# Holding up-projection blocks in PSUM and rounding all sigmoid pieces on ScalarE in a one-core FFN kernel

## The reference, cut to what matters

```python
def act_qdq(x):
    scale = jnp.maximum(jnp.max(jnp.abs(x)) / qmax, 1e-12)      # qmax = 32767
    return jnp.clip(jnp.round(x / scale), -qmax - 1.0, qmax) * scale
def fixed_qdq_u16(x):
    return jnp.clip(jnp.round(x * 65536), 0.0, 65535.0) / 65536
x = act_qdq(x)                                    # (16, 128, 128): 2048 tokens of 128
up = act_qdq(x @ lpbq_dequant(w_up).T)            # 384 wide
gate = act_qdq(x @ lpbq_dequant(w_gate).T)
sig = fixed_qdq_u16(jax.nn.sigmoid(gate))
gate = act_qdq(gate * sig)
o = act_qdq(gate * up)
return o @ lpbq_dequant(w_down).T
```

## Time and profile before

| | |
|---|---|
| Median of 3 runs | 301.76 us (301.69 to 303.23) |
| Span of the profiled execution, first to last instruction | 301.2 us |
| Median less this span | 0.56 us |
| TensorE busy | 264.4 us (88%) |
| VectorE busy | 258.8 us (86%) |
| ScalarE busy | 215.6 us (72%) |
| GpSimd busy | 76.2 us (25%) |
| Chain that ended last | TensorE 79%, VectorE 16% of the span |

### The profile page before, as it was taken

How to read it: one execution, slowest core, us unless ns; L and a number is a source line. 1 busy time by engine, 2 the same in 40 slices (tenths; PEclk the granted TensorE clock), 3 DMA queues, 4 the chain that set the end, 5 groups by cost and what they waited for, 6 DMA issues and landing times.

```text
span 301.2 us, 8834 instructions
## 1 busy us (share of the span) xinstructions
PE 264.4 (88%) x2716; PEld 205.5 (68%) x2716; DVE 258.8 (86%) x635; ACT 215.6 (72%) x455; POOL 76.2 (25%) x148
## 2 busy tenths in 40 slices
PE   4969940049989999999999999999999999999994
PEld 4824440016956777778888788888777887888874
DVE  4888999989898897779988799887799988889885
ACT  6367899998842677767777676667566766689892
POOL 3367997000025413011302112212110311101000
PEclk9989976557999999999999999999999999999999
DMA  6990443101500000000000000000001000001000
GB/s 186 314 310 4 84 94 76 28 0 35 90 17 2 0 3 1 0 2 2 19 0 0 2 3 26 2 0 0 1 2 30 8 0 0 2 1 37 0 2 27
DMA packets 24031, 10.63 MB, mean 35 GB/s; under 512 B 13355, under 2 KB 22982, under 8 KB 24006
## 3 DMA queue, kind: packets, MB, share of 16 engines
q1 hardware_dynamic: 23470, 10.05, 13.6%
q10 hardware_dynamic: 536, 0.26, 0.3%
HBM read 6.11 MB, written 1.05 MB: 24 GB/s over the span
## 4 chain that ended last, share of the span: by engine, by line
PE 79%; DVE 16%; issue 1%; ACT 1%; DMA 1%; SPq 0%; DVEq 0%
PE bank L893 78%; DVE peak L706 3%; DVE big L728 3%; DVE peak L633 2%; DVE big L711 1%; DVE big L744 1%; PE bank L937 1%; DMA y_sb<-in_cond 1%; PE bank L1017 0%; DVE big L746 0%; DVE wyT L779 0%; DVE pkm L626 0%; DVE big L738 0%; DVE x_sb L759 0%; DVE q L700 0%
## 5 line engine op out<-in xcount | busy, mean ns | idle before, releaser
L893 PE MATMUL bank<-big,wt 128*128 128x384 f16 (+2 forms) x480 | 124.8, 336 | 0.6 <-DVE big L872 0.5
L893 PE MATMUL bank<-wt,big 128*128 (+1 forms) x1536 | 111.5, 219 | 0.1
L872 DVE TENSOR_TENSOR big<-big 128x384 f16<-128x384 f32 (+2 forms) x160 | 93.2, 585 | 20.5 <-ACT big L594 16.1
L893 PEld LDWEIGHTS bank<-wt,big 128*128 128x128 f16 x1536 | 97.9, 97 | 16.2 <-issue 0.2
L592 ACT ACTIVATE big<-bank,miscT 128x384 f32<-128x384 f32 (+2 forms) x160 | 96.2, 602 | 15.3 <-PE bank L893 8.2
L893 PEld LDWEIGHTS bank<-q,wxh 128*128 128x128 f32 x254 | 44.4, 189 | 17.4 <-issue 3.4
L893 PEld LDWEIGHTS bank<-big,wt 128*128 (+1 forms) x480 | 50.0, 117 | 4.8 <-issue 1.1
L580 ACT ACTIVATE q<-bank (+1 forms) x112 | 20.6, 184 | 38.7 <-PE bank L893 37.9
L404 POOL CAST big<-q 128x64 f16<-128x64 f32 x32 | 13.2, 413 | 129.0 <-ACT q L580 126.5
L868 DVE CAST big<-big 128x512 f16<-128x512 f32 (+2 forms) x104 | 38.6, 372 | 4.8 <-ACT big L592 3.9
L827 DVE SCALAR_TENSOR_TENSOR wyT<-bank,gates,wyT 128x128 f32<-128x128 f32 x128 | 39.8, 343 | 1.0 <-issue 0.6
(11 more groups left out here) (165 smaller groups left out, 320.0 us busy)
## 6 DMA issues: line engine op xcount, KB each, us to landing
wnat<-in_w SPq DMA_DIRECT2D x8, 512.0 KB, 7.7
x_sb<-in_x SPq DMA_DIRECT2D x4, 256.0 KB, 4.3
out_block<-wyT SPq DMA_DIRECT2D x15, 64.0 KB
wn<-in_w_gate ACTq DMA_DIRECT2D x1, 192.0 KB, 4.9
wn<-in_w_up SPq DMA_DIRECT2D x1, 192.0 KB, 5.6
wn<-in_w_down SPq DMA_DIRECT2D x1, 192.0 KB, 5.7
b_in<-in_b SPq DMA_DIRECT2D x12, 4.0 KB
wt<-wyT SPq DMA_TRANSPOSE x8, 3.0
```

The source lines that it names most:

```text
L872: V.tensor_tensor(g_lo[:, par, f, 0:w], g32[:, f, 0:w], g_hi[:, par, f, 0:w], ALU.subtract).then_inc(g_lo_done, 1)
L893: return nc.tensor.matmul(o, l, r, start=start, stop=stop, skip_group_check=True)
```

## The change

- Only the first 17 of the 24 projection blocks are copied out by ScalarE. The last seven, up blocks m = 5 to 11, stay in banks 0, 1, 2, 5, 6, 3 and 4 (`HELD_BANKS`). VectorE takes their maxima from there, one by one; ScalarE rounds them out of the bank into `up2`.
- All six sigmoid pieces are rounded by ScalarE; `round_sigmoid` on VectorE is gone, and so the up scale has no `meanwhile`.
- Up is rounded in six pieces of 1024; a piece with a held block takes two instructions of 512, ten in all. VectorE's products wait for their own piece.
- TensorE's transposes of x come after the last up piece and behind `spread_peak(3)`, and `take_xT` stands between the later roundings on ScalarE. The Gelu table is loaded after these.
- `weight_lo(2)` on VectorE comes right after the gate scale, and TensorE's block 23, which goes to its bank 4, waits for it.

```diff
@@ -54,8 +54,9 @@
 CHUNK_OF = [c for c in range(CH) for _ in range(TILES[c])]
 LAST_SYNC, LAST_SCALAR = (0, 2), (1,)
 LATE = NK - ACC_SCALAR
-SIG_V = 2
 B2_ROWS = CTILES * E
+UP_OUT = 5
+UP_HELD = NJ * NK - UP_OUT
 GATE_UP = 2.0 ** 18
 
 
...
@@ -179,6 +180,7 @@
         DOWN_BANKS = [1, 2, 3, 4, 5]
         ACC_BANKS = [6, 7, 1, 2]
         GU_BANKS = [5, 6, 0, 1, 2]
+        HELD_BANKS = [GU_BANKS[(NJ * NK + m) % 5] if m < 10 else 3 + m - 10 for m in range(UP_OUT, NJ * NK)]
         W0_BANKS = [4, 3, 4]
         W_BANKS = [0, 5]
         MISC_AT = NJ * P
@@ -208,6 +210,18 @@
 
         def sixth(t, n):
             return t[:, TOK // 2 * n:TOK // 2 * (n + 1)]
+
+        def up_bank(m):
+
+            return banks[HELD_BANKS[m - UP_OUT]]
+
+        def up_pieces():
+
+            return [[(b, b % NK * NJ + b // NK) for b in (2 * n, 2 * n + 1)] for n in range(2 * NJ)]
+
+        def up_steps(n):
+
+            return sum(1 if all(m < UP_OUT for _, m in piece) else len(piece) for piece in up_pieces()[:n])
 
         def tokens(t, k):
 
@@ -500,7 +514,7 @@
                 A(blk(qhi, k), c32[:, 4 * k:4 * k + 4, :].rearrange("p b l -> p (b l)"), ACT.Copy,
                   bias=-MAGIC).then_inc(q_hi_s, 1)
 
-            for n in range(2 * NJ * NK):
+            for n in range(NJ * NK + UP_OUT):
                 act.wait_ge(gu_mm, n + 1)
                 t, k, j = (gate2, up2)[n // (NJ * NK)], n % (NJ * NK) // NJ, n % NJ
                 A(blk(t, j * NK + k), banks[GU_BANKS[n % 5]][:, :], ACT.Copy).then_inc(gu_sb, 1)
@@ -516,22 +530,24 @@
                 A(sixth(gate2, n), sixth(gate2, n), ACT.Copy, scale=sc[:, 1, 4:5], bias=MAGIC).then_inc(gateq, 1)
                 act.wait_ge(gateq, n + 1)
                 A(sixth(sig2, n), q16(sixth(gate2, n)), ACT.Sigmoid, scale=sc[:, 1, 2:3]).then_inc(sig_done, 1)
-                if n >= SIG_V:
-                    act.wait_ge(sig_done, n + 1)
-                    A(q16(sixth(sig2, n), U16), sixth(sig2, n), ACT.Copy, scale=65536.0).then_inc(sig_16, 1)
+                act.wait_ge(sig_done, n + 1)
+                A(q16(sixth(sig2, n), U16), sixth(sig2, n), ACT.Copy, scale=65536.0).then_inc(sig_16, 1)
 
             act.wait_ge(scale_done, 3)
-            for n in range(NJ):
-                A(third(up2, n), third(up2, n), ACT.Copy, scale=sc[:, 2, 4:5], bias=MAGIC).then_inc(upq, 1)
-            nc.scalar.preload_act_table(ACT.Gelu)
-            for k in range(2):
-                take_xT(k)
+            for n, piece in enumerate(up_pieces()):
+                if all(m < UP_OUT for _, m in piece):
+                    A(sixth(up2, n), sixth(up2, n), ACT.Copy, scale=sc[:, 2, 4:5], bias=MAGIC).then_inc(upq, 1)
+                    continue
+                for b, m in piece:
+                    src = blk(up2, b) if m < UP_OUT else up_bank(m)[:, :]
+                    A(blk(up2, b), src, ACT.Copy, scale=sc[:, 2, 4:5], bias=MAGIC).then_inc(upq, 1)
 
             act.wait_ge(scale_done, 4)
             for n in range(1, 2 * NJ):
                 A(sixth(sig2, n), sixth(sig2, n), ACT.Copy, scale=sc[:, 3, 4:5], bias=MAGIC).then_inc(g2q, 1)
-                if n <= 2:
-                    take_xT(n + 1)
+                if n <= NK:
+                    take_xT(n - 1)
+            nc.scalar.preload_act_table(ACT.Gelu)
             act.wait_ge(wt_t[0], 16 * W_POOL)
             weight_hi(W_POOL)
             for i in range(W_POOL, W_CHUNKS - 1):
@@ -706,33 +722,34 @@
                 link(V.tensor_reduce(peak[:, i, k:k + 1], tokens((gate2, up2)[i - 1], k), XY, ALU.max,
                                      apply_absolute_value=True))
 
-            def round_sigmoid(n):
-                dve.wait_ge(sig_done, n + 1)
-                V.tensor_scalar(sixth(sig2, n), sixth(sig2, n), SIG_MAX, SIG_MAGIC, ALU.min, ALU.add).then_inc(sig_round, 1)
-
-            for i in (1, 2):
-
-                for k in range(i - 1, NK):
-                    peak_gate_up(i, k)
-                    if i == 1 and k == 0:
-                        weight_lo(1)
-                    if i == 2 and k == 2:
-                        weight_lo(2)
-                peak_to_scale(i, NK, lambda u: link(V.tensor_scalar(u, sc[:, 0, 2:3], 1.0 / WS, None, ALU.mult)),
-                              (lambda: peak_gate_up(2, 0)) if i == 1 else (lambda: round_sigmoid(0)))
+            def peak_up(first, to):
+                for m in range(first, to):
+                    dve.wait_ge(gu_mm, NJ * NK + m + 1)
+                    link(V.tensor_reduce(peak[:, 2, m - 3:m - 2], up_bank(m)[:, :], X, ALU.max,
+                                         apply_absolute_value=True))
+
+            for k in range(NK):
+                peak_gate_up(1, k)
+                if k == 0:
+                    weight_lo(1)
+            peak_to_scale(1, NK, lambda u: link(V.tensor_scalar(u, sc[:, 0, 2:3], 1.0 / WS, None, ALU.mult)),
+                          lambda: peak_gate_up(2, 0))
+            weight_lo(2)
+            dve.wait_ge(gu_sb, NJ * NK + UP_OUT)
+            link(V.tensor_reduce(peak[:, 2, 1:2], tokens(up2, 1)[:, 0:2, :], XY, ALU.max, apply_absolute_value=True))
+            peak_up(UP_OUT, NJ * NK)
+            peak_to_scale(2, 2 + UP_HELD, lambda u: link(V.tensor_scalar(u, sc[:, 0, 2:3], 1.0 / WS, None, ALU.mult)))
 
             for n in range(2 * NJ):
-                if 0 < n < SIG_V:
-                    round_sigmoid(n)
-                dve.wait_ge(*((sig_round, n + 1) if n < SIG_V else (sig_16, n - SIG_V + 1)))
+                dve.wait_ge(sig_16, n + 1)
                 V.tensor_tensor(sixth(sig2, n), q16(sixth(gate2, n)), q16(sixth(sig2, n), U16), ALU.mult).then_inc(g2_done, 1)
                 dve.wait_ge(g2_done, n + 1)
                 block_peak(3, n, sixth(sig2, n))
             peak_to_scale(3, 2 * NJ, lambda u: link(V.tensor_scalar(u, sc[:, 1, 2:3], 1.0 / 65536.0, None, ALU.mult)))
 
             link(V.tensor_scalar(sixth(sig2, 0), sixth(sig2, 0), sc[:, 3, 4:5], MAGIC, ALU.mult, ALU.add))
-            dve.wait_ge(upq, NJ)
             for n in range(2 * NJ):
+                dve.wait_ge(upq, up_steps(n + 1))
                 if n > 0:
                     dve.wait_ge(g2q, n)
                 V.tensor_tensor(sixth(up2, n), q16(sixth(sig2, n)), q16(sixth(up2, n)), ALU.mult).then_inc(p_done, 1)
@@ -949,7 +966,9 @@
                     pe.wait_ge(*((q_hi_s, Q_HI_SCALAR.index(k) + 1) if k in Q_HI_SCALAR else (q_hi_v, k + 1)))
                 if n == 4:
                     pe.wait_ge(cq_done, 3)
-                if n >= 5:
+                if n == 2 * NJ * NK - 1:
+                    pe.wait_ge(wT_done, 3)
+                if 5 <= n < NJ * NK + 10:
                     pe.wait_ge(gu_sb, n - 4)
                 if n == W0_AT[1]:
                     pe.wait_ge(cq_done, NK)
@@ -959,16 +978,16 @@
                 if n == NJ * NK + 6:
                     spread_peak(1)
                 w = NJ * t + j
-                mm3(banks[GU_BANKS[n % 5]][:, :], wT_hi[:, w, :], wT_lo[:, w, :], blk(qhi, k), blk(qlo, k),
+                o = banks[GU_BANKS[n % 5]] if n < NJ * NK + UP_OUT else up_bank(n - NJ * NK)
+                mm3(o[:, :], wT_hi[:, w, :], wT_lo[:, w, :], blk(qhi, k), blk(qlo, k),
                     r_lo_ready=(q_done, k + 1) if t == 0 and j == 0 else None).then_inc(gu_mm, 1)
-            pe.wait_ge(gu_sb, 2 * NJ * NK)
             spread_peak(2)
-            pe.wait_ge(wT_done, 3)
+            spread_peak(3)
+            pe.wait_ge(upq, up_steps(2 * NJ))
             for k in range(NK):
                 for b in range(4 * k, 4 * k + 4):
                     last = nc.tensor.transpose(banks[1 + k][:, P * (b % 4):P * (b % 4 + 1)], x_sb[:, b, :], ident[:, :])
                 last.then_inc(xT_mm, 1)
-            spread_peak(3)
 
             def keep_busy(n):
 
```

More of the change, by code:

```diff
@@ L159, in program @@
         pk_part, pk_all, scale_done, dve_step, pool_step = sems("pk_part pk_all scale_done dve_step pool_step")
-        gu_mm, gu_sb, gateq, upq, sig_done, sig_round, sig_16, g2_done, g2q, p_done, oq, o_hi_done, o_lo_done, o_lo_p = sems(
-            "gu_mm gu_sb gateq upq sig_done sig_round sig_16 g2_done g2q p_done oq o_hi_done o_lo_done o_lo_p")
+        gu_mm, gu_sb, gateq, upq, sig_done, sig_16, g2_done, g2q, p_done, oq, o_hi_done, o_lo_done, o_lo_p = sems(
+            "gu_mm gu_sb gateq upq sig_done sig_16 g2_done g2q p_done oq o_hi_done o_lo_done o_lo_p")
         down_mm, x1_done, x1_hi_done, x1_lo_done, x1T_mm = sems("down_mm x1_done x1_hi_done x1_lo_done x1T_mm")
```

## The result

The changed kernel took 305.03 us in the median of 7 runs (303.96 to 306.75), the kernel before 302.41 on the same chips (301.69 to 303.23): a ratio of 1.0077, 95% interval 1.0054 to 1.0100. By the ratio it is slower by 2.3 us (the medians lie 2.6 apart), against +0.8 forecast, and 305.03 lies above the stated range, which ended at 304.5.

A forecast was written before the change was run, and what follows sets the result against it. The start of TensorE's weight chunks, where warming and ScalarE's first `weight_hi` meet, was taken as the bound. ScalarE's -3.0 + 2.7 + 0.9 + 0.1 + 0.1 = +0.8 on 301.76 gave 302.6 us, range 301.0 to 304.5.

The forecast's parts named there:

- meeting point: Start of TensorE's weight chunks, which need ScalarE's first `weight_hi`: 72.2 to 72.3 forecast against 71.39, +0.8 to +0.9 us.
- rival A: VectorE's chain sets the end, if ScalarE reaches `weight_hi` before 70 us: at best 300.6 us; chance 0.10.
- steps 1 to 3: ScalarE: seven PSUM copies go, -3.0 us; two more sigmoid roundings, +2.7; up in ten instructions, +0.9, through at 62.9.
- step 4: ScalarE's five roundings and four copies of x, 7.13 us, start at 62.9; the scale they need stands at 62.1.
- 0.8 us of slack: On ScalarE, between the scale of gate times sigmoid at 62.1 and the start of the roundings needing it at 62.9.
- step 5: ScalarE's Gelu table load, 1.28 us, moves behind the roundings and copies of x at the same cost; +0.12 for waiting.
- rival C: The table load on ScalarE costs more in its new place, a second cost of that size: +2.1, 303.9 us; chance 0.06.
- The sum's last step: Eight TensorE chunks at the old pace put the spread of the last maximum at 80.4; the +0.8 reaches the end.
- Rival B: TensorE idles 2.9 us after warming and falls to the lower clock as chunks start: 303.9 to 305.2 us; chance 0.18.

The follow-up runs named there:

- the kernel before with the three moves: The kernel before with the first two high halves made early, Gelu table loaded after the second low byte, 8 warming matmuls: 302.47 us, ratio 1.0001.

## Why the prediction was wrong

Point by point, with after's numbers against the forecast:

- *What bounds the kernel.* Right. The meeting point, start of the weight chunks, decided, and rival A (VectorE's chain) didn't: VectorE idled 4.80 us for the spread, and moving the start of the chunks alone, with VectorE's work as it was, took the whole loss away.
- *ScalarE, steps 1 to 3.* Right to 0.1 us: gate rounding 0.04 behind its scale (34.06, 34.10); six trips 34.10 to 55.39, 21.3; up pieces through at 62.20, 6.8 us.
- *ScalarE, step 4.* Failed in the profiled execution. "0.8 us of slack" was a wait of 0.67. VectorE's maxima were right (40.89 - 30.85 = 10.0 against 9.1, +0.93 for +0.83), but the products took 60.73 - 42.97 = 17.8 instead of 16.3. I had kept the overlap cost with GpSimd at what the old positions gave, 1.87, 1.51 and 1.51; in their new position they gave 1.94, 2.21 and 2.21, and in the execution with more warming 1.39, 1.51 and 2.21, near the forecast: that position is partly chance. The prediction named these multiplications only as a possible gain.
- *ScalarE, step 5, and rival C.* The load took 1.28 and the next instruction began 0.01 after it. C is refuted, and no second cost stands in either place. Nor does a drain of 1.38 us, which the Trainium skill, in "ScalarE: Activation LUTs", What ACT_TABLE_LOAD costs, counts with each load; the 1.28 us of the load itself agree.
- *TensorE.* The transposes ran from 62.26, warming from 65.43 at the full clock (0.95 in the slice from 65 us), after 19 us of idle and then only the two matmuls of a spread and those transposes. That speaks against what the Trainium skill says in "TensorE: Matmul & The Clock Gate", Part 4, of transpose mode, for these fp32 transposes; the rows call them MATMUL, and no row shows the mode.
- *Meeting point.* +1.4 measured in the profiled pair, for +0.8 forecast; the difference is step 4's wait. In the execution with more warming, where ScalarE didn't wait, it was +1.0. This part of the sum was mis-sized by little.
- *The sum's last step* failed, and it is the step that made the forecast wrong: "eight chunks at the old pace". (Six of the eight stand before the spread; the pace, 8.2 us for them, was read rightly.) They took 11.3 us in the profiled execution, since TensorE idled 3.50 us before them and its clock had fallen to 1.2 GHz. Rival B had the mechanism, the place (idle from 68.6 to 72.1) and the price (2.6 at most; 3.1 in the profiled execution), with a chance of 0.18. It should have been the likeliest case. The argument against it, that a late rise shortens the idle, was weak: by its own sum TensorE was free from 69.3 and ScalarE late by up to 2.9 us. And the 2.8 us of idle that B leaned on came from one row; a fall followed 1.90 us in another kernel. In the median the clock's share is 1.0 us, taken as what more warming gave back.
- *The base.* 301.76 was the median of three; the kernel before stood at 302.41 with the changed kernel's runs and at 302.6 to 302.7 in all later sets.

## What to carry to other kernels

Warm-up work on TensorE and the arrival of its first input must end together: here an input that came 1.4 us later cost 3.1 us more behind it, since TensorE idled and then began its real work at half clock. Before moving work onto an engine, ask what stands at the end of its queue and who waits for that; here two instructions, moved ahead of a block they didn't depend on, were worth all 2.3 us, and neither shift of work between ScalarE and VectorE paid, alone or together. A price read beside another engine's work holds only at that position, and the position itself moved by 1 us between executions of the same code.

## What the runs showed of the hardware

VectorE's two-input product and GpSimd's subtraction, both with their operands in SBUF, take turns: 1.22 us alone, 2.21 when it meets a whole subtraction, 1.39 to 1.51 when it meets the end of a step of GpSimd's, and GpSimd's 0.62 becomes 1.59. VectorE's reductions beside such subtractions kept their 1.22 (in the kernel before, the one at 49.54 beside the subtraction at 50.06). The Trainium skill says the same in "SBUF — State Buffer", SBUF: two separate sides: a port pair that GpSimd and a VectorE instruction with two SBUF inputs hold for a whole instruction, the other blocking. The trace agrees: the product at 46.20, begun 0.03 us behind a subtraction of 1.15, took 0.99 us more than alone, and the reductions, with one input, weren't hit.

The granted clock rose to 2.4 GHz near 65.0 us, 2.8 us after the transposes began, in the changed kernel, and 4.8 us after they began in the run with more warming. It fell with idles of 3.50, 3.01, 1.90 and 1.89 us, yet not with ones of 2.87 and 1.59 (the kernel before with the three moves). The chunks' quarter step took 0.64 us at 1.2 GHz and 0.335 at 2.4.
